# Gating the state sums: copied by ScalarE and multiplied by GpSimd, in place of VectorE from the banks

## What is computed

```
def step(hst, ins):
    dt_t, B_t, C_t, x_t = ins
    dA = jnp.exp(dt_t[:, :, None] * A)
    hst = hst * dA + (dt_t * x_t)[:, :, None] * B_t[:, None, :]
    y_t = jnp.einsum('bds,bs->bd', hst, C_t)
    return (hst, y_t)
...
y = jnp.swapaxes(ys, 0, 1) + xs * Dskip
return y * jax.nn.silu(z) @ out_w
```

## Time and profile before

| | us |
|---|---|
| median of 3 runs | 3247.95 (3247.91 to 3250.06) |
| profiled execution | 3246.55 |
| its span | 3244.7 |
| TensorE busy | 3181.8 |
| VectorE busy | 2845.3 |
| ScalarE busy | 2805.9 |
| GpSimd busy | 2338.9 |

### The profile page before, as it was taken

How to read it: one execution, slowest core, us unless ns; L and a number is a source line. 1 busy time by engine, 2 the same in 40 slices (tenths; PEclk the granted TensorE clock), 3 DMA queues, 4 the chain that set the end, 5 groups by cost and what they waited for, 6 DMA issues and landing times.

```text
span 3244.7 us, 59428 instructions
## 1 busy us (share of the span) xinstructions
PE 3181.8 (98%) x22634; PEld 2506.4 (77%) x22634; DVE 2845.3 (88%) x2848; ACT 2805.9 (86%) x4627; POOL 2338.9 (72%) x1128
## 2 busy tenths in 40 slices
PE   7999999999999999999999999999999999999899
PEld 4888998999999989998998999899888542222244
DVE  3989999999999999999999999999999578888121
ACT  6999999999999999999999999999999436777620
POOL 1989999999999999899999999998999220000000
PEclk9999999999999999999999999999999999999999
DMA  4323222222222222222222222222222043422000
GB/s 130 87 83 95 76 68 74 68 72 68 73 69 95 69 71 76 72 70 72 75 72 69 71 68 74 69 71 68 87 66 71 33 98 64 74 34 33 13 7 20
DMA packets 208319, 220.95 MB, mean 68 GB/s; under 512 B 84353, under 2 KB 158081, under 8 KB 207777
## 3 DMA queue, kind: packets, MB, share of 16 engines
q1 hardware_dynamic: 208034, 217.14, 23.6%
HBM read 196.38 MB, written 18.20 MB: 66 GB/s over the span
## 4 chain that ended last, share of the span: by engine, by line
PE 72%; ACT 16%; DVE 5%; issue 4%; POOL 3%; DMA 0%; DVEq 0%; ACTq 0%; SPq 0%
PE psum L1701 19%; PE psum L1469 16%; PE psum L1695 14%; PE psum L1692 11%; ACT arena L1131 7%; ACT arena L1113 5%; PE psum L1778 4%; PE psum L1767 3%; DVE arena L1359 3%; POOL arena L824 3%; PE psum L1752 3%; DVE row_max L1422 1%; PE psum L1721 1%; ACT arena L1156 1%; ACT arena L960 0%
## 5 line engine op out<-in xcount | busy, mean ns | idle before, releaser
L1359 DVE TENSOR_TENSOR_SCAN arena<-arena,psum 128x512 f32<-128x512 f32 x2048 | 2370.6, 1228 | 57.2 <-PE psum L1695 42.9
L824 POOL TENSOR_TENSOR arena<-arena 128x1024 f32<-128x1024 f32 x1024 | 2218.1, 2183 | 223.4 <-DVE arena L1359 201.1
L1131 ACT ACTIVATE arena<-arena,a_neg 128x512 f32<-128x512 f32 x2048 | 1434.5, 722 | 33.9 <-PE psum L1695 33.3
L1701 PE MATMUL psum<-ident,arena 128*128 128x128 f32 x8192 | 1229.3, 273 | 1.7 <-POOL arena L824 1.7
L1113 ACT ACTIVATE arena<-arena,bT 128x512 f32<-128x512 f32 x1536 | 1107.3, 721 | 0.0
L1695 PE MATMUL psum<-ident,arena 128*128 128x128 f32 x6144 | 1006.8, 273 | 0.0
L1701 PEld LDWEIGHTS psum<-ident,arena 128*128 128x128 f32 x8192 | 960.1, 141 | 2.1 <-POOL arena L824 2.1
L1692 PE MATMUL psum<-arena 128*128 128x128 f32 x4096 | 817.0, 281 | 15.0 <-ACT arena L1113 9.7
L1692 PEld LDWEIGHTS psum<-arena 128*128 128x128 f32 x4096 | 646.2, 191 | 225.7 <-issue 148.4
L1695 PEld LDWEIGHTS psum<-ident,arena 128*128 128x128 f32 x6144 | 741.8, 142 | 0.0
L1469 PE MATMUL psum<-arena 128*128 128x512 f32 (+1 forms) x1440 | 672.2, 588 | 8.7 <-DVE arena L1231 2.9
(11 more groups left out here) (120 smaller groups left out, 860.2 us busy)
## 6 DMA issues: line engine op xcount, KB each, us to landing
arena<-bc_dram SPq DMA_DIRECT2D x256, 512.0 KB, 3.7
arena<-diag_dram SPq DMA_DIRECT2D x240, 128.0 KB, 2.1
arena<-qk_dram SPq DMA_DIRECT2D x96, 128.0 KB
diag_dram<-arena SPq DMA_DIRECT2D x32, 256.0 KB, 4.3
qk_dram<-arena SPq DMA_DIRECT2D x8, 768.0 KB, 3.5
arena<-in_x SPq DMA_DIRECT2D x4, 512.0 KB, 10.3
arena<-skip_w SPq DMA_DIRECT2D x64, 32.0 KB, 2.0
arena<-sums_dram SPq DMA_DIRECT2D x64, 32.0 KB, 1.8
```

The lines of the kernel that those rows point to most:

```text
L824: pool.tensor_tensor(out[:, :, way], h_now[:, :, way], c_row, ALU.mult)\
L1131: act.activation(decay[:, w % AHEAD, f], dt_[:, u % 2, f], ACT.Exp, scale=a_neg[:, d, f, st:st + 1])\
L1359: dve.tensor_tensor_scan(hs[:, w % RING, f, rows][:, way], decay[:, w % AHEAD, f, way], psum[:, 4 + n % U_BANKS, way], end_state(w - DS, f ...
L1701: return pe.matmul(psum[:, c, f * P:(f + 1) * P], hs[:, w % RING, f, at:at + P], ident[:, :], is_transpose=True, start=False, stop=w % DS ...
```

## The change

ScalarE copies the four banks into `dtxT` of the unit that has ended, behind step 2 (`copy_y`). GpSimd multiplies the copies with the gates in SBUF, one behind each of steps 3, 6, 9 and 12, and in unit 7 behind each of steps 2, 3, 4 and 5. `first_state` waits for the copy (`y_copied`) where it waited for the gate. In units 1 to 6 the slots 4 to 19 now hold `xs` and `zs` in turn, two slots each, and the four turns `yT` come at slots 20 to 23. The gating behind unit 7 stays on VectorE.

```diff
@@ -52,6 +52,7 @@
 TURNS = ("yT", "bT", "dtxT")
 SLIDE = -(-DS // RING)
 PIECES = {"out": 4, "bc": 4, "dt": 4, "down": 4}
+Y_COPY_STEP, GATE_STEPS, LAST_GATE_STEPS = 2, (3, 6, 9, 12), (2, 3, 4, 5)
 SILU_STEP, LAST_SILU_STEP = 24, 23
 DT_STEPS = {"exp": 4, "ln": 5, "softplus": 6}
 DTX_STEPS = (40, 44, 53, 55)
@@ -205,7 +206,7 @@
             tile_full tile_free_act tile_free_dve
             centred squared rstd_step rstd_ready normed h_ready
             exp_step dt_ready dtx_ready skip_w_ready bc_rows_ready a_exp a_ready silu_ready
-            dve_const uT_ready u_full decay_ready scan_done prod_done reduce_done gated
+            dve_const uT_ready u_full decay_ready scan_done prod_done reduce_done y_copied gated
             x_updated
             scores_full scores_free max_step top_ready top_full top_copied rows_in
             hi_ready mid_ready lo_ready qk_out ones_set stack_in_0 stack_in_1 stack_in_2
@@ -288,7 +289,7 @@
                 place(zs_[:1] + steps("mean", "ln0", 2) + zs_[1:2] + xs_[:1] + steps("sum", "ln0", 2) + steps("mean", "ln0", 3)
                       + xs_[1:3] + steps("sum", "ln0", 3) + xs_[3:] + zs_[2:], 0)
             else:
-                place([step for k in range(NI) for step in (xs_[k], yT_[k], zs_[k])], 4)
+                place([step for k in range(NI) for step in (xs_[k], zs_[k])] + yT_, 4)
             at[BC_TURN] = ("bc", u + 1)
             at[BT_TURN] = ("bT", u + 1)
             for f in range(NI):
@@ -795,6 +796,14 @@
                     pool.tensor_scalar(out[:, c], out[:, c], mods[:, k, C + c, b:b + 1], mods[:, k, c, b:b + 1], ALU.mult, ALU.add)\
                         .then_inc(s["h_ready"], 1)
 
+            def gate_steps(u):
+                return GATE_STEPS if u < UNITS - 1 else LAST_GATE_STEPS
+
+            def gate_y(u, c):
+
+                pool.wait_ge(s["y_copied"], TB * u + c + 1)
+                pool.tensor_tensor(gates[u % 2][:, c], dtxT[:, u % 2, c], gates[u % 2][:, c], ALU.mult).then_inc(s["gated"], 1)
+
             def finish_dt(u, f):
 
                 pool.wait_ge(s["exp_step"], exp_steps(u) + 3 * (f + 1))
@@ -829,6 +838,8 @@
                     back = TURN[u].get(st - 2)
                     if back and back[0] == "sum":
                         scale(*back[1:])
+                    if u and st in gate_steps(u):
+                        gate_y(u - 1, gate_steps(u).index(st))
                     if st in DTX_STEPS and u < UNITS - 1:
                         make_dtx(u + 1, DTX_STEPS.index(st))
 
@@ -1116,6 +1127,12 @@
                     act.activation(diag[:, w // 2 % DIAG_PAIRS, w % 2], ident[:, :], ACT.Copy, scale=bT[:, 0, c, st:st + 1])\
                        .then_inc(s["uT_ready"], 1)
 
+            def copy_y(u, c):
+
+
+                act.wait_ge(s["reduce_done"], NI * (u + 1) * DS)
+                act.activation(dtxT[:, u % 2, c], psum[:, c], ACT.Copy).then_inc(s["y_copied"], 1)
+
             act.preload_act_table_set(EXP_LN)
             for c in range(TB):
                 scan_input(0, c)
@@ -1132,6 +1149,9 @@
                            .then_inc(s["decay_ready"], 1)
                         if w + 1 < SCAN_TILES:
                             scan_input(w + 1, f)
+                    if u and st == Y_COPY_STEP:
+                        for c in range(TB):
+                            copy_y(u - 1, c)
                     do(act_turns(u, st))
                     if any(step[0] in ("silu", "silu up") for step in act_turns(u, st)):
                         act.preload_act_table_set(EXP_LN)
@@ -1360,10 +1380,6 @@
                                                psum[:, 4 + n % U_BANKS, way],
                                                end_state(w - DS, f) if hi else 0.0, op0=ALU.mult, op1=ALU.add)\
                            .then_inc(s["scan_done"], 1)
-                        if u and st == 1 and f:
-                            gate_y(u - 1, f - 1)
-                        if u and st == 2 and f == 0:
-                            gate_y(u - 1, NI - 1)
                     do(dve_turns(u, st))
             for f in range(NI):
                 gate_y(UNITS - 1, f)
@@ -1713,7 +1729,7 @@
 
                 u = w // DS
                 if u:
-                    pe.wait_ge(s["gated"], TB * (u - 1) + c + 1)
+                    pe.wait_ge(s["y_copied"], TB * (u - 1) + c + 1)
                 if c == 0:
                     pe.wait_ge(s["skip_w_ready"], 2 * NI)
                     pe.wait_ge(s["prod_done"], 2 * (w + 1))
```

## The result

The changed kernel took 3269.97 us (median of 4 runs, 3267.89 to 3272.43), the kernel before 3248.65 beside it. The ratio is 1.0065, with an interval of 1.0053 to 1.0077, so it is 21 us slower. I had forecast 3266, 18 us slower.

A forecast was written before the change was run, and what follows sets the result against it. TensorE, 98% busy, was taken as the bound from each unit's first-state products to step 24. Heads 4.6, silus 9.6 and last unit 3.6 sum to 17.8, rounded to 18 us slower: 3266.0 us, range 3255 to 3272.

The forecast's parts named there:

- TensorE is the bound behind the head, so VectorE's 17 us buy nothing: From first-state products to step 24 TensorE sets the pace; removing VectorE's 28 gates, 17 us, gains nothing.
- Heads, 4.6: At heads of units 1 to 6, first-state products wait for ScalarE's first copy: 4.6 us slower together.
- The turns behind the gate tiles, 9.6: In units 1 to 6, turns placed later make the silus 1.6 us later each: 9.6 us slower.
- GpSimd's multiplies free in units 1 to 6: GpSimd's gates behind steps 3, 6, 9 and 12 are worked off before the turns at slot 20: no cost.
- The last unit, 3.6: In unit 7 TensorE's first turn waits 4.4 us longer for GpSimd's four gates; the scan comes 3.6 us later.
- T + 27.6: Unit 7: GpSimd's fourth gate ends 27.6 us after T, TensorE's first-state start, put at 2221.0; so at 2248.6.
- The terms' own bounds: Whole kernel: 16 us with silus at 1.3, to 20 with silus at 1.8 and no VectorE slack in the last unit.
- the three terms: Losses at the heads (4.6 us), at the silus of units 1 to 6 (9.6) and in the last unit (3.6).
- contention: Rival, chance 0.08: GpSimd's gates hold up the scans; 20.6 us more in odd units, 3287, or 3302 with all 28.
- the silus don't come later: Rival, chance 0.10: ScalarE finds time between steps 20 and 24, so only 8 us remain, 3256.
- the gain: Rival, chance 0.05: VectorE decides at the unit heads, and the 17 us come back, 3231.
- nothing to measure: Rival, chance 0.05: gain at the heads and loss at the silus cancel, within about 0.2%, 6.5 us.

The follow-up runs named there:

- E7: Changed kernel with copies and GpSimd gates moved and slots ordered xs, zs, yT four times; 3249.70 us beside 3249.76 for the kernel before.
- E1: Kernel before with only the slot order changed: turns at slots 20 to 23 in units 1 to 6, VectorE still gating; 3256.71 us, ratio 1.0029.
- E4: Changed kernel with extra ScalarE work behind the copies at each head, where one table load of 1.28 us ran; 3271.81 us, ratio 1.0073.
- E5: Changed kernel without GpSimd's 24 multiplies in units 1 to 6, leaving those sums ungated; 3273.4 us, ratio 1.0073.
- E2: Changed kernel, but VectorE gates the sums of unit 6 from the banks as before; 3264.61 us, ratio 1.0052.
- E3: Changed kernel, but the four copies at the head of unit 1 stand behind step 1 of ScalarE, not step 2; 3265.58 us, ratio 1.0053.
- E6: Changed kernel with unit 1's copies behind step 1 and unit 6's sums gated by VectorE, slot order still changed; 3260.99 us, ratio 1.0038.

## Why the prediction was right

*TensorE is the bound behind the head, so VectorE's 17 us buy nothing.* Right but for a small part. The chain of unit 1 was read as that of all units, odd and even. In the kernel before, TensorE's steps 3 and 4 take 9.2 us in unit 3 (first products of steps 3 and 5 at 1004.75 and 1013.95) and 8.75 in unit 2 (700.81 and 709.56). With the gates gone from VectorE they take 8.75 in unit 3 too, in the changed kernel and in E7, while E1, which keeps the gates, still takes 9.2. So 0.45 us came back in unit 3, and the same in unit 5, and the time from first state to silus grew by 1.1 there, not by 1.6. VectorE has no gap there in the kernel before (eight scans in 9.47 us from 1002.84), so TensorE seems to wait for the banks that the scans read; no row names that wait, and it is not shown further.

*Heads, 4.6.* Right: 3.0, 1.1 and 1.1 at units 1, 3 and 5, and -0.1 at 2, 4 and 6, make 4.8. The copies themselves cost ScalarE nothing (E4).

*The turns behind the gate tiles, 9.6.* Right in mechanism and size: 9.4 alone (E1), 8.5 within the change, since units 3 and 5 gave 0.5 each back.

*GpSimd's multiplies free in units 1 to 6.* Right (E5).

*The last unit, 3.6.* The mechanism was right, TensorE waiting for the fourth gate until T + 27.3 (2263.41 - 2236.1) where I had T + 27.6. The size was 4.6, all of which E2 took away; the term left out the half clock.

*The clock.* This is the step that was missing. I priced a wait of TensorE as its length. At each of the two long ones the clock fell to half for 3.4 us, and together with the stretch in unit 2 it made 3.3 us in units 1 and 2. In unit 7 the wait and the clock were only taken away together. Of its 4.6 us about 1 is the clock's by my estimate, which is the rest over the 3.6 forecast for the wait; a further 3.4 us at half clock cost 1.4 to 1.5 there (E3, E4). The sum is then 4.8 + 8.5 + 3.3 + 4.6 = 21.2, against 21.3 in the scan.

*The range.* The terms' own bounds were 16 to 20 us, 3264 to 3268, and the measured 21.3 us and 3269.97 lie above them. The time is within the range because its end was set at 3272, for which I had no reason from the rows. The direction and the three terms came out by the mechanisms named; that the missing clock of some 4 us still fitted in was luck.

The rivals: contention fell with E5, "the silus don't come later" with E1, the gain and "nothing to measure" with the result, which is slower clear of noise. As for the Trainium skill: GPSIMD Engine Reference, Engine selection, says that GpSimd takes about twice as long for an elementwise operation with two inputs. The trace agrees: 1.29 against 0.67 for VectorE's gates, which had one input in PSUM, and 0.69 for VectorE's four multiplies of this shape with both in SBUF (L1248 of the kernel before). It mattered only where a queue waited behind it. The Trainium skill (SBUF — State Buffer, Who interferes with whom) says that a VectorE instruction with at most one SBUF input, outside the two-port modes, does not contend with GpSimd. The scans have one of their two inputs in PSUM, and the trace agrees: 1230 ns a scan beside 1228 before, 1.24 us for the 61 scans that overlap one of GpSimd's gates, and no gain in units 1 to 6 without the gates (E5).

## What to carry to other kernels

Work taken from an engine that is nearly full is worth little if another engine's chain sets the pace at that place; look for the engine with no gaps there, and then for who must arrive before it. Changing the order of a sum of equal work is not free: what counts is how much of it stands ahead of the next point at which engines wait for each other, here the two silus. And where a new wait stops TensorE for several microseconds, look at the granted clock and price the wait above its length: here the 3.9 us wait cost 1.6 us more than it delayed the first-state product.

## What the hardware showed that I had not expected

Of each kernel one execution was profiled. The four profiles with TensorE's matmuls standing still for 3.9 us at the head of unit 1 (the changed kernel, E2, E4, E5) all had 3.4 us at half clock right there, and the other four (E1, E3, E6 and E7) had none, nor had the kernel before. The same holds for the 4.5 us in unit 7: half clock in the changed kernel and in E3, E4 and E5 (3.4 us twice, 6.8 us twice), none in E1, E2, E6 and E7. Each 3.4 us at half clock cost about 1.6 us in units 1 and 2: unit 1 lost 6.2 us with it and 4.6 of that is explained by the late start and the order, and unit 2 lost 3.2 with it and 1.5 without (E3). The stretch in unit 2, behind waits of 1.3 and 1.1 us, came in just those four profiles that had one in unit 1; like waits in units 4 and 6 never brought one, nor did they in unit 2 of E1, E3 and E6. Why it comes in unit 2 alone was not settled.
